# Second attention layer: VectorE turns of 32x32 blocks and 64 small matmuls per step, GpSimd inverts the softmax sums itself

## What is computed

```python
for i in range(2):                       # two halves of 128 positions, weights of their own
    h = einsum('od,bdl->bol', Wqkv[i], z1ss[:, :, s:e]) + einsum('od,bdl->bol', Winj[i], u1ss[:, :, s:e])
...
q, k, v = jnp.split(w_heads, 3, axis=1)  # 16 heads x 64 each
rq = q + r_w_bias
score = einsum('bndi,bndj->bnij', rq, k) * SCALE
prob = jax.nn.softmax(score, axis=-1)
attn_vec = einsum('bnij,bndj->bndi', prob, v)
attn_out = einsum('od,bdl->bol', Wo, attn_vec) + bo[None, :, None]
x = attn_out + z1ss
...                                      # layer norm over the 128 features
```

## Time and profile before

| | us |
|---|---|
| median of 3 runs | 1515.6 (1515.39 to 1516.03) |
| span of the profiled execution | 1515.6 |
| PE busy in it | 1330.7 (88%) |
| DVE busy | 1003.3 (66%) |
| ACT busy | 888.4 (59%) |
| POOL busy | 649.5 (43%) |
| second layer | from 640 to 1390 |

### The profile page before, as it was taken

The page is one execution under the profiler, slowest core; times in us unless marked ns, Lnnn a source line. Parts: engine busy times, 40 slices in busy tenths (PEclk is TensorE's granted clock), DMA queues, the critical chain, the costliest instruction groups (busy, mean ns, idle before and its releaser), DMA issues. The chain is left out here.

```text
span 1515.6 us, 29849 instructions
## 1 busy us (share of the span) xinstructions
PE 1330.7 (88%) x9586; PEld 999.7 (66%) x9586; DVE 1003.3 (66%) x2031; ACT 888.4 (59%) x3038; POOL 649.5 (43%) x615
## 2 busy tenths in 40 slices
PE   4678898898989776589999999999999999996897
PEld 2444565565656454478888888888888888884464
DVE  3477777777777844376666666676676667664354
ACT  2476767677776734365656656555565555553443
POOL 3487676766666632023334333333333333342000
PEclk9899999999999998789999999999999999998899
DMA  4030000000000000010000000000000000000110
GB/s 158 1 140 18 5 15 3 14 10 7 10 7 3 11 0 1 28 43 2 8 1 9 0 0 7 0 7 0 0 7 0 7 0 0 2 1 1 51 42 28
DMA packets 18509, 24.54 MB, mean 16 GB/s; under 512 B 1360, under 2 KB 16912, under 8 KB 18064
## 3 DMA queue, kind: packets, MB, share of 16 engines
q1 hardware_dynamic: 18448, 23.77, 4.8%
HBM read 21.67 MB, written 2.10 MB: 16 GB/s over the span
## 5 line engine op out<-in xcount | busy, mean ns | idle before, releaser
L953 POOL TENSOR_TENSOR prob<-prob,l_z_inv 128x512 f32<-128x512 f32 x256 | 261.2, 1042 | 457.2 <-DVE l_z_inv L1194 457.2
L1113 ACT ACTIVATE prob<-psum,l_neg_max 128x256 f32<-128x256 f32 x512 | 236.0, 473 | 240.5 <-DVE l_neg_max L1188 240.5
L618 ACT ACTIVATE ring_e<-ring_e,neg_max 128x128 f32<-128x128 f32 x512 | 199.4, 395 | 98.8 <-DVE neg_max L758 98.3
L409 POOL TENSOR_TENSOR ring_e<-ring_e,z_inv 128x512 f32<-128x512 f32 x128 | 174.2, 1361 | 139.5 <-DVE z_inv L753 139.5
L1188 DVE TENSOR_REDUCE l_neg_max<-psum 128x2 f32<-128x512 f32 x256 | 163.9, 682 | 10.6 <-PE psum L1007 10.6
L1035 PE MATMUL psum<-pT,vs 128*64 128x256 f32 x1024 | 138.8, 391 | 6.7 <-DVE aTl L1204 6.7
L1019 PEld LDWEIGHTS psum<-ident,prob 128*128 128x128 f32 x1024 | 109.8, 141 | 49.0 <-issue 45.4
L1019 PE MATMUL psum<-ident,prob 128*128 128x128 f32 x1024 | 139.9, 280 | 0.0
L521 PE MATMUL psum<-ident,ring_e 128*128 128x128 f32 x512 | 85.7, 292 | 50.7 <-ACT ring_t L625 49.7
L1199 DVE COPY pT<-psum 128x512 f32<-128x512 f32 x128 | 88.1, 689 | 51.0 <-PE psum L1019 51.0
L521 PEld LDWEIGHTS psum<-ident,ring_e 128*128 128x128 f32 x512 | 55.8, 144 | 81.5 <-issue 77.3
(11 more groups left out here) (196 smaller groups left out, 3510.3 us busy)
## 6 DMA issues: line engine op xcount, KB each, us to landing
wz_raw<-wz_in SPq DMA_DIRECT2D x2, 1536.0 KB, 10.4
x_in<-x SPq DMA_DIRECT2D x8, 256.0 KB, 2.7
cT<-ctxT SPq DMA_DIRECT2D x8, 256.0 KB, 2.7
w<-w_in SPq DMA_DIRECT2D x2, 1024.0 KB, 11.5
l_ub<-ctx_in SPq DMA_DIRECT2D x8, 256.0 KB, 2.8
cg<-ctx_in SPq DMA_DIRECT2D x4, 512.0 KB, 3.5
out<-fin SPq DMA_DIRECT2D x4, 512.0 KB, 2.8
wi_raw<-wi_in SPq DMA_DIRECT2D x1, 1536.0 KB, 15.2
```

The source lines that it names most:

```text
L409: pool.tensor_tensor(p, p, z_inv[:, n % RE, :].unsqueeze(2).broadcast_to([P, QUAD, P]), ALU.mult)\
L618: last = nc.scalar.activation(e, e, ACT.Exp, bias=neg_max[:, n % RE, h:h + 1], accum_out=z_sum[:, n % RE, h:h + 1])
L953: pool.tensor_tensor(e, e, z_inv[:, t % RE, h, :].unsqueeze(2).broadcast_to([P, 2, D]), ALU.mult)\
L1113: last = nc.scalar.activation(prob[:, t % RE, h, qt * D:(qt + 1) * D], score_bank[h][:, qt * D:(qt + 1) * D], ACT.Exp, bias=neg_max[:, t % ...
```

## The change

All of it is in `layer1`.

- The transposes on PE go, and so do both copies out of the turn banks. DVE turns the probabilities itself, in 32x32 blocks: `nc.vector.transpose` on 128x512, once per head. Block `c` of quarter `a` of the rows then holds 32 keys of 32 queries, with the keys on partitions `32a` to `32a + 31`.
- `times_v` becomes 64 matmuls per step: for each of 8 groups of 32 keys, 4 quarters of rows and 2 heads, 32 rows by 64 columns of the array and 64 moving columns. The quarters write into four PSUM banks. ACT and DVE read the four banks in one instruction each and put the queries back in order.
- The values must lie on each quarter of the partitions. ACT copies v to `vs` (one buffer), SP writes it to device memory (`l1_values`) and reads it back four times per step into `vr`, which has four buffers (`RV`).
- q and k are plain fp32 and are no longer split: the scores are 4 fp32 matmuls a step (8 passes) instead of 12 fp32r matmuls. ACT alone moves q, k and v out of PSUM.
- POOL waits for the exponentials, makes the inverse of the sums by `pow` with minus one, waits for it and multiplies. DVE's reciprocals go.
- The output projection is no longer summed in a bank of its own, but in four blocks of two pairs (`o0` to `o3`, six matmuls each) in the work banks; DVE adds each block to `part`. `o3` is done in step 2 of the next round. `FILLS` moves some names: `k0+` from step 14 to 15, `v3b0` from 10 to 11, `k7` from 11 to 12.

```diff
-            def turn(i, t):
...
-                            last = nc.tensor.transpose(turn_bank[h][:, kt * D + qt * P:kt * D + (qt + 1) * P],
...
+                for h in range(2):
+                    pe.wait_ge(*turned.at(i, 2 * t + h))
+                pe.wait_ge(*spread_in[t % RV].at(i, t // RV))
+                pe.wait_ge(*aT_lo.at(i, t - 1))
+                for c in range(KEYS):
+                    for a in range(QUARTERS):
+                        rows = slice(a * SQ, (a + 1) * SQ)
                         for h in range(2):
...
+                            last = mm(pv_banks[a][h * HD1:(h + 1) * HD1, :],
+                                      vr[rows, t % RV, c, h * HD1:(h + 1) * HD1],
+                                      pT[rows, h, :].rearrange("p (t c r) -> p t c r", t=2, r=SQ)[:, :, c, :],
+                                      start=c == 0, stop=c == KEYS - 1)
...
+            def save_values(i, g, b):
+                tile = g * NB + b
+                sp.wait_ge(*work.out(f"v{g}b{b}", i))
+                for t in (4 * g + b, 4 * g + NB + b):
+                    sp.wait_ge(*spread_in[t % RV].at(i - 1, t // RV))
+                sp.dma_start(values[tile].rearrange("(c p) f -> p c f", p=P), vs[:, :, :])\
+                    .then_inc(values_out.sem, 16)
+
+            def spread_values(i, t):
+                pair, b = divmod(t, NB)
+                tile = pair // 2 * NB + b
+                sp.wait_ge(*values_out.at(i, tile))
+                sp.wait_ge(*pv_done.at(i, t - RV))
+                at = pair % 2 * 2 * HD1
+                src = values[tile][:, at:at + 2 * HD1].rearrange("(c s) f -> s c f", s=SQ)
+                for a in range(QUARTERS):
+                    sp.dma_start(vr[a * SQ:(a + 1) * SQ, t % RV, :, :], src).then_inc(spread_in[t % RV].sem, 16)
...
             def norm(i, t, h):
+                pool.wait_ge(*exp_done.at(i, 2 * t + h))
+                pool.tensor_tensor(z_inv[:, t % RE, h, :], z_sum[:, t % RE, h, :], minus_one[:, :], ALU.pow)\
+                    .then_inc(z_inv_done.sem, 1)
                 pool.wait_ge(*z_inv_done.at(i, 2 * t + h))
...
-            def copy_turned(i, t):
-                dve.wait_ge(*turned.at(i, 2 * t + 1))
+            def turn(i, t, h):
+                dve.wait_ge(*probs_done.at(i, 2 * t + h))
                 dve.wait_ge(*pv_done.at(i, t - 1))
-                nc.vector.tensor_copy(pT[:, 1, :], turn_bank[1]).then_inc(copied[1].sem, 1)
+                nc.vector.transpose(pT[:, h, :], prob[:, t % RE, h, :]).then_inc(turned.sem, 1)
```

More of the change, by code:

```diff
@@ L879, in layer1 @@
         made = [n for n in names if n[0] in "qkv" and n != "var"]
-        split = [n for n in made if n[0] in "qk"]
-        work = Banks(ctx, nc, "l1_work", names, [psum[:, 5 + j, :] for j in range(2)])
+        work = Banks(ctx, nc, "l1_work", names, [psum[:, 6 + j, :] for j in range(2)])
         events += work.full_ev + work.out_ev
-        work_hi = event("work_hi", len(split))
         u_in = event("u_in", 1, 16)
@@ L943, in _, with body @@
             sp.dma_start(wo_raw[:, :, :], v["wo_in"].rearrange("(h r) o -> r h o", r=P)).then_inc(wo_in, 16)
[L944 to L946 removed]
+            def save_values(i, g, b):
[14 more added lines that the diff above has]
+                    sp.dma_start(vr[a * SQ:(a + 1) * SQ, t % RV, :, :], src).then_inc(spread_in[t % RV].sem, 16)
+            def body(i, last):
+                for g in range(H1 // 4):
+                    for t in range(4 * g, 4 * g + 4):
+                        if t % 4 < NB:
+                            save_values(i, g, t % 4)
+                        spread_values(i, t)
+                    if g == 2 and not last:
+                        sp.wait_ge(*zu_lo.at(i, 1))
+                        load_u(i + 1)
+            for i in range(R1):
+                body(i, i == R1 - 1)
+            sp.wait_ge(*values_out.at(R1 - 1, H1 // 4 * NB - 1))
+            for t in range(STEPS - RV, STEPS):
+                sp.wait_ge(*spread_in[t % RV].at(R1 - 1, t // RV))
         @block.gpsimd
@@ L1024, in times_v @@
-            def times_v(i, t):
-                pair, b = divmod(t, NB)
-                if t % 4 < 2:
-                    pe.wait_ge(*work.out(f"v{pair // 2}b{b}", i))
-                for h in range(2):
-                    pe.wait_ge(*copied[h].at(i, t))
-                pe.wait_ge(*aT_lo.at(i, t - 1))
-                for kt in range(2):
-                    for h in range(2):
-                        at = (2 * (pair % 2) + h) * HD1
-                        last = mm(pv_bank[h * HD1:(h + 1) * HD1, :], vs[:, pair // 2 % 2, b, kt, at:at + HD1],
-                                  pT[:, h, kt * D:(kt + 1) * D], start=kt == 0, stop=kt == 1)
-                last.then_inc(pv_done.sem, 1)
@@ L1048, in mean @@
-            def mean(i, name):
-                pe.wait_ge(*work.free(name, i))
-                pe.wait_ge(*y_done.at(i))
+                    for h in range(2):
+                        rows = slice(h * HD1, (h + 1) * HD1)
+                        last = mm(score_bank[h][:, qt * D:(qt + 1) * D], q[rows, pair % 2, qt, b, :],
+                                  k[rows, pair % 2, :, b, :], start=True, stop=True)
+                        if qt == 1:
+                            last.then_inc(scores_done.sem, 1)
@@ new lines, in times_wo @@
+            def times_wo(i, name, m):
+                slots = (0, 1) if m % 2 == 0 else (2, 3)
+                pe.wait_ge(*work.free(name, i))
+                pe.wait_ge(*aT_lo.at(i - 1 if m == 3 else i, 4 * m + 3))
+                for slot in slots:
+                    for wp, ap in ((0, 0), (0, 1), (1, 0)):
+                        last = mm(work.psum(name), wo[wp][:, 2 * m + slot % 2, :],
+                                  aT[ap][:, slot, :, :].rearrange("p b d -> p (b d)"),
+                                  start=(slot, wp, ap) == (slots[0], 0, 0), stop=(slot, wp, ap) == (slots[1], 1, 0))
+                last.then_inc(work.fills(name), 1)
@@ L1051, in mean @@
+            def mean(i, name, product):
+                pe.wait_ge(*work.free(name, i))
+                pe.wait_ge(*work.out(product, i))
                 mm(work.psum(name), mean_w[:, :], y[:, :, :].rearrange("p b d -> p (b d)"),
@@ L1288, in body @@
                         if is_made(name):
-                            rest_work(r, name)
+                            continue
+                        if name == "o3" and first:
+                            dve.wait_ge(*work.full(name, i))
+                            nc.vector.memset(y[:, :, :], 0.0).then_inc(work.reads(name), 1)
+                        elif name[0] == "o":
+                            add_product(r, name, int(name[1]))
                         elif name == "mean":
```

204 lines of the change are left out of this document (80 added, 124 removed).

## The result

| | before | after |
|---|---|---|
| median, us | 1515.8 (1515.4 to 1516.4, 4 runs) | 1598.0 (1593.4 to 1601.7, 4 runs) |
| ratio | | 1.054, 95% interval 1.051 to 1.057 |
| profiled span, us | 1515.6 | 1597.2 |
| a round of the second layer, us | 91.27 | 101.9 (mean of five) |

What follows compares the result with a forecast made beforehand. TensorE was taken to bound the second layer (90.13 of 91.27 us a round); minus 8.2 us a round on it, plus 2.2 of new waits, gave minus 6.0, over eight rounds minus 48: 1515.6 to 1468 us, range 1440 to 1555.

Steps and rivals of the forecast that it cites:

- Transposes leave PE, -0.85 a step: TensorE, each step of the second layer: eight transposes go, minus 0.85 us.
- scores 1.06: TensorE, scores of each step: plain fp32 in four pairs of passes takes 1.06 us, plus 0.15 us.
- turns 0.69: VectorE, two 32x32 transposes of 128x512 per step: taken at 0.69 us each, at worst 1.38.
- power 0.70: GpSimd, inverting the sums by a power: 0.70 us per half, at worst 1.01.
- GpSimd near 56 us a round: GpSimd's busy time in a middle round: near 56 us in place of 33.6.
- GpSimd's latency: GpSimd ahead of VectorE's transpose: 0.5 us more per half, costing nothing while steps last 4 us or more.
- The output projection at nothing: TensorE, output projection: the same 24 products in four blocks instead of eight, costed at nothing.
- new waits +2.2: Per round: 1.3 us around step 13, 0.3 for k0, 0.6 for the values; plus 2.2 us.
- The product, 1.15 us: TensorE, product with the values in each step: 64 overlapping small matmuls take 1.15 us, plus 0.13 us.
- rival 2: Each step's 64-matmul product costs more than it replaces: decides from 1.58 us; 1550 at 1.9 us, near 1790 unoverlapped; chance 0.17.
- Code: TensorE's longer loop no longer fits its instruction memory; the forecast's sum gave the fetching no cost.
- Rival 3: Code fetch in the second layer's rounds: some 20 packets, 24 us a round; half exposed, 96 us back, 1564; chance 0.09.

Runs made afterwards that it cites:

- the power alone: The kernel before, with only GpSimd waiting for the exponentials and inverting the sums by pow, VectorE's reciprocals gone: 1522.0 us (1.001).
- the bf16 kernel: The changed kernel with probabilities and values in bf16, each of the 64 matmuls one pass: 1429.2 us; with the rounds written out, 1416.9 us.
- the test of the product alone: The changed kernel plus stretches of twelve products ahead of the layer's last product: 1.59 us a product in a loop, 3.72 written out; no kernel time given.

## Why the prediction was wrong

- **Transposes leave PE, -0.85 a step; scores 1.06; turns 0.69; power 0.70; GpSimd near 56 us a round.** Right, each by its row (1.07, 0.691, 0.697, and 282.1 / 5 = 56.4 us). GpSimd's latency costs nothing, as the power alone showed in the kernel before.
- **The output projection at nothing, new waits +2.2.** Right or too careful: with four matmuls as product the round is 2.5 us shorter than the forecast. The values' landings take 3.2 us instead of 2.2, and the waits for them 1.2 us a round instead of 0.6.
- **The product, 1.15 us.** The first step that failed: 1.52. The lower bound took the array (16 passes of 58 ns), and 8 ns of issue per pair from four records that start inside 32 ns. Four that start together after a switch say little about a long row of them (perhaps they stood ready; no run shows why): over 128 pairs it is 11 to 12 ns. The term is worth 0.37 x 16 x 8 = 47 us. The result stood near rival 2's own point, 1.58 us, from which the change gains nothing.
- **Code.** The second step that failed. The forecast left the fetch out and made it a rival with a chance of 0.09: 20 packets a round (22 came), 1.2 us each, half of it exposed, 96 us. That the code would be late was right: it costs 6.3 + 1.6 + 3.7 = 11.6 us a round, some 93 us (an estimate). That 96 lies so near is luck. Rival 3 let every packet expose half of its 1.2 us; what the runs show is a few gaps of 1.3 to 2.7 us, a supply of 3.7 us a packet, and a loss of clock that the rival didn't have. The reason given for hiding it ("hidden while the next is fetched during a step of 5 us") was wrong in its premise, because a step does not use its code evenly. One product of 1.5 us uses a whole packet, and a packet comes every 3.7 us. The row to weigh was not the mean over a round but the densest 256 instructions.
- **The sum.** Rivals 2 and 3 were priced one at a time, each against the forecast. Both came: 1468 + 47 + 93 = 1608, against 1598. The rest of the forecast was 2.5 us a round too slow, 20 us, and the waits for `vr` give about 5 of it back, so the sum holds to some 10 us and no better. The range ended at one of the two alone.
- **The lower clock** behind the gaps, 3.7 us of those 11.6, stood in no step.

What stays open: why the gap in step 14 is 2.7 us where 3.7 less 1.5 would leave 2.2 or less, and why with half the product ahead of the scores gaps of 3.2 us remain. The packets' times show where to look: in step 14 the transfer starts within 0.2 us of PE's stop (1044.16, stop at 1044.09), in step 9 0.9 us ahead of it (1014.40, stop at 1015.28). Why it is asked for so late no run shows. That a gap ends when a packet has come is shown by these times; that gaps fall where a border between packets lies late in a product is only read off from where they stand (behind 117 of 128 passes in step 9) and from how they moved with 24 instructions.

## What to carry to other kernels

When a change multiplies an engine's instructions, price two things apart from its arithmetic: the issue of each (here 11 to 12 ns for a load with its pass, with 32 columns as with 64), and the supply of code if the loop no longer fits, which was 3.7 us per 256 instructions where they are used up fastest. A list that doesn't fit cost nothing where every 256 loads and passes lasted longer than that (14 us and more in the kernel before, 4.2 in the bf16 kernel, both written out); a jump back costs as well. When rivals don't exclude each other, the range must reach to their sum.

## What was not expected of the hardware

- Code arrives at 3.7 us per packet of 16 KB with idle DMA engines; the packet itself is on a DMA engine for about 1.2 us, and PE goes on 1.2 to 1.7 us after it has landed.
- Behind gaps of 2.0 and 2.7 us inside a product the granted clock was 0.63 and 0.67 over the next 4 to 5 us, with 0.50 (1.2 GHz) in the first of them, so these gaps cost 3.5 and 4.0 us. In the test of the product alone, PE ran at 0.50 for over 200 us of small matmuls.
- Eight tiles of 32 rows and 64 columns overlap: 11 to 12 ns a pass among them at full clock, 83 ns (at half clock) when one tile is used at a time.
- Reads of 4 KB pieces land no earlier than reads of 512-byte pieces: 3.1 us for 128 KB either way.
